# The head of a two-layer network as a third woven stream instead of four barriered phases

## The reference, cut to what matters

```python
x = L0_attn_x                                   # (8, 512, 128)
xn = _layernorm(x)
s = _L0_attn_ref(xn, Wq, Wk, Wv, Wo)            # causal attention, 16 heads, key width 8, value width 64
g = _silu(_L0_ffn_ref(xn, w_gate, c_fc, c_proj))# 8 experts, top 2, at most 512 tokens per expert
x = x + s * g
xn = _layernorm(x)
s = _L1_attn_ref(xn, ...)                       # delta rule in chunks of 32, mixed with an EMA
g = _silu(_L1_ffn_ref(xn, ...))                 # two layers of windowed attention and a gated ffn
x = x + s * g
```

## Time and profile before

| what | us |
|---|---|
| median of 3 runs (2751.47 to 2760.95) | 2754.06 |
| the profiled execution's own time | 2756.0 |
| its span, first to last instruction | 2754.2 |
| PE busy | 2051.2 (74%) |
| ACT busy | 1416.9 (51%) |
| DVE busy | 1352.0 (49%) |
| POOL busy | 532.1 (19%) |

### The profile page before, as it was taken

How to read it: one execution, slowest core, us unless ns; L and a number is a source line. 1 busy time by engine, 2 the same in 40 slices (tenths; PEclk the granted TensorE clock), 3 DMA queues, 4 the chain that set the end, 5 groups by cost and what they waited for, 6 DMA issues and landing times.

```text
span 2754.2 us, 51642 instructions
## 1 busy us (share of the span) xinstructions
PE 2051.2 (74%) x20756; PEld 1166.5 (42%) x20756; DVE 1352.0 (49%) x3140; ACT 1416.9 (51%) x3619; POOL 532.1 (19%) x601
## 2 busy tenths in 40 slices
PE   1405574779787978798878887898789787978767
PEld 0303223444453445344634463445444453445434
DVE  2512333554546463746474646555654546463442
ACT  0311361387537662776367735764477537762433
POOL 0270200312022110402040304020302022110220
PEclk9957776789888988898889897998889888988787
DMA  5362300200020001100020002000200020000000
GB/s 187 102 173 64 77 2 12 48 2 2 13 52 1 2 7 34 24 3 5 14 47 3 1 14 51 3 1 13 51 2 2 13 52 1 2 7 12 1 0 5
DMA packets 97224, 75.91 MB, mean 28 GB/s; under 512 B 44451, under 2 KB 87804, under 8 KB 94814
## 3 DMA queue, kind: packets, MB, share of 16 engines
q1 hardware_dynamic: 92894, 66.35, 9.7%
q0 software_dynamic: 4096, 6.32, 1.5%
HBM read 41.55 MB, written 33.16 MB: 27 GB/s over the span
## 4 chain that ended last, share of the span: by engine, by line
PE 45%; ACT 16%; DVE 14%; issue 8%; POOL 5%; DMA 1%; SPq 0%; POOLq 0%; DVEq 0%; ACTq 0%
PE PS L945 5%; PE PS L1581 4%; ACT work_a L1146 4%; PE PS L1616 4%; ACT work_b L1812 3%; PE PS L1718 3%; POOL work_b L2021 3%; DVE work_a L1265 3%; PE PS L1689 3%; PE PS L1731 2%; DVE work_a L1309 2%; PE PS L921 2%; PE PS L1651 2%; ACT work_a L1163 2%; PE PS L1680 2%
## 5 line engine op out<-in xcount | busy, mean ns | idle before, releaser
L1146 ACT ACTIVATE work_a<-PS,work_a 128x512 bf16<-128x512 f32 (+3 forms) x512 | 263.4, 530 | 79.3 <-DVE work_a L1265 77.8
L2021 POOL TENSOR_TENSOR work_b<-work_b,tables 128x256 f32<-128x256 f32 x256 | 212.0, 848 | 450.7 <-DVE work_b L1908 450.7
L1812 ACT ACTIVATE work_b<-PS,neg_max 128x192 f32<-128x192 f32 (+1 forms) x512 | 201.9, 417 | 121.1 <-DVE neg_max L1948 75.0
L1265 DVE TENSOR_REDUCE work_a<-PS 128x2 f32<-128x1024 f32 (+3 forms) x256 | 200.8, 821 | 106.5 <-PE PS L897 103.6
L1163 ACT ACTIVATE work_a<-PS 128x1024 f32<-128x1024 f32 (+1 forms) x192 | 169.6, 883 | 121.2 <-PE PS L927 119.1
L1581 PE MATMUL PS<-wqkv,hT 128*128 128x512 f32 x384 | 200.6, 654 | 7.5 <-DVE work_b L1908 6.2
L1616 PE MATMUL PS<-k,q 64*128 64x192 f32 (+1 forms) x1024 | 162.3, 454 | 58.7 <-ACT shiftT L1798 27.9
L2035 POOL TENSOR_TENSOR rstd_b<-var_eps_b,minus_half 128x4 f32<-128x4 f32 x16 | 16.4, 1027 | 876.1 <-DVE var_eps_b L121 876.1
L945 PE MATMUL PS<-work_a 128*64 128x512 f32 (+3 forms) x1024 | 179.8, 454 | 0.0
L1616 PEld LDWEIGHTS PS<-k,q 64*128 64x128 f32 x1024 | 109.7, 266 | 112.2 <-ACT work_b L1812 39.8
L1828 ACT ACTIVATE work_b<-PS 128x768 f32<-128x768 f32 (+1 forms) x128 | 97.2, 759 | 97.6 <-PE PS L1659 97.6
(11 more groups left out here) (295 smaller groups left out, 4218.4 us busy)
## 6 DMA issues: line engine op xcount, KB each, us to landing
work_a<-stack_d SPq DMA_DIRECT2D x32, 512.0 KB, 9.6
stack_d<-parts SPq DMA_DIRECT2D x48, 192.0 KB, 3.5
stack_d<-parts SPq DMA_DIRECT2D x32, 128.0 KB, 2.7
x_all<-in_L_attn_x_dram SPq DMA_DIRECT2D x4, 512.0 KB
slots_in<-xn_all SPq DMA_DIRECT2D x1, 2048.0 KB, 9.4
xnT_d<-xnT_all SPq DMA_DIRECT2D x1, 2048.0 KB
xn_all<-slots_in SPq DMA_DIRECT2D x8, 256.0 KB, 3.4
slots_out<-xn_all SPq DMA_DIRECT2D x8, 256.0 KB, 2.2
```

Source lines behind the costliest of these rows:

```text
L1146: nc.scalar.activation(dump0[:, n % 2 * T:n % 2 * T + (i + 1) * P], PS[:, a:a + (i + 1) * P], ACT.Exp, bias=neg_max0[:, k:k + 1], accum_ou ...
L1265: nc.vector.reduce_max(neg_max0[:, 2 * g * NT + i:(2 * g + 2) * NT:NT], at[:, :, Q_AT[i]:Q_AT[i] + (i + 1) * P], AX_X, negate=True).then_i ...
L1812: nc.scalar.activation(dump2[:, n % 4 * 256:n % 4 * 256 + w], PS[:, a:a + w], ACT.Exp, bias=neg_max2[:, k:k + 1], accum_out=sums2[:, k:k + ...
L2021: nc.gpsimd.tensor_tensor(to[:, n, :, r, :], src[:, n, :, 1 - r, :], table(2 * n + 1, t)[:, 32 * r:32 * r + 32].unsqueeze(1).to_broadcast( ...
```

## The change

- The barriers and the two loops go. Setup, norms, routing, scatter, stacks and experts are a third stream H of 45 slices: 1 of loads, 8 of norms (one batch each), 1, 3 of routing, 7 of stacks (batches 1 to 7), 1, and 24 of experts (three for each).
- H is woven with stream A of batch 0 by `HEAD_AHEAD`: slices 0 to 11 of H come first, then 30 slices of A (v, the whole first pass, unit 0 of the second), slice 12 of H, 4 of A, and then slices 13 to 20 of H with 1, 1, 1, 0, 1, 0, 4 slices of A ahead of slices 14 to 20. Slices 21 to 44, the experts, have one slice of A among them. Then A goes on with unit 14 of its second pass.
- SP loads x and five small tensors first, then clears, presets, and the other 43 loads. Batch 0's stack is written within the norms. The 2 MB store of `xnT_d` is split into batch 0 and the rest.
- The stack parts have two buffers instead of four; every batch's q and k go through banks 5 and 6 of PSUM instead of three pairs.
- For batch 0, the gather, its weighting and the additions move from the beginning of attention to behind its second pass, after all eight experts are stored, and gather into an area of its own.
- The conversions of masks and the rotary tables move from setup to slice 12 of H, behind the first 30 slices of A.
- `x1`, `y`, `out1` of the odd batches, and all of stream B's work area, share memory with the head.
- `A_AHEAD` has other values with the same sum; `A_AHEAD[0]` stays 17.
- The last barrier goes too.

```diff
+        FIRST_LOADS = [(cst[:, :], const_in[:, 0:C_LOOP]), (head_c[:, :], const_in[:, C_LOOP:C_COS]),
+                       (qk_in[:, 0:P], w_q0), (qk_in[:, P:2 * P], w_k0), (wg[:, :], w_gate)]
+        def head_sp(sp):
+            for q in range(4):
+                sp.dma_start(xn_all[...], x_in[...]).then_inc(sh["x_in_%d" % q], 16)
+                if q == 0:
+                    for dst, src in FIRST_LOADS:
+                        sp.dma_start(dst, src).then_inc(sh["loaded_first"], 16)
+            sp.wait_ge(sh["zeros"], 1)
+            for q in range(8):
+                sp.dma_start(slots_in.rearrange("(q p r) f -> q p (r f)", q=8, p=P)[q], zeros[:, :]
+                             ).then_inc(sh["cleared"], 16)
...
+            for dst, src in LOADS:
+                sp.dma_start(dst, src).then_inc(sh["loaded"], 16)
+            yield
...
+            for b in range(B):
+                if b == 1:
+                    sp.wait_ge(sh["T_copied"], 1)
+                    sp.dma_start(xnT_d[0:P, :], xnT_all[:, 0:T]).then_inc(sh["first_stored"], 16)
+                if b == 2:
+                    stacked(0)
+                yield
...
+            for b in range(1, B):
+                stacked(b)
+                yield
...
+            sp.wait_ge(sh["qk"], 2 * B)
+            sp.wait_ge(sh["xnT_stored"], 16)
+            for e in range(2):
+                weights(e)
+            for n in range(RING):
+                sp.wait_ge(stack_written[n], 16 * 12 * (B // RING))
+            sp.wait_ge(scattered, 16 * 2 * NTILE)
+            for e in range(2):
+                rows_of(e)
+            yield
...
+        def head_act(act):
+            def parts(b):
+                if b >= 2:
+                    act.wait_ge(stack_written[(b - 2) % RING], 16 * 12 * ((b - 2) // RING + 1))
...
+        def head_pool(gp):
...
+            gp.wait_ge(sh["slot"], 3)
+            gp.wait_ge(sh["cleared"], 16 * 9)
+            for n in range(NTILE):
+                for k in range(2):
+                    nc.gpsimd.indirect_dma_start(...).then_inc(scattered, 16)
+            gp.wait_ge(sh["converted"], 1)
...
         def attention_pool(gp, b):
...
             if b:
                 gp.wait_ge(sd["mixed"], ofd("mixed"))
+                gather()
...
+            for n in range(UNITS + 1):
+                yield
+            if b == 0:
+                gp.wait_ge(sh["stored"], 16 * NE)
+                gather()
+                weighted()
+                added()
...
         def attention_sp(sp, b):
+            if b == 0:
+                sp.wait_ge(sh["first_stored"], 16)
+                sp.wait_ge(sh["preset"], 64)
+            if b == 1:
+                sp.wait_ge(sh["xnT_stored"], 16)
+            sp.wait_ge(stack_written[b % RING], 16 * 12 * (b // RING + 1))
...
         A_LEAD = 76
-        A_AHEAD = (17, 0, 2, 1, 0, 0, 0, 0, 0, 4, 2, 0, 2, 0, 1, 0, 0, 0, 2, 2, 2, 1, 2, 1, 2, 1, 2, 2, 1, 6, 3, 0, 1, 1,
-                   1, 1, 2, 3, 1, 2, 1, 2, 1, 1, 1, 1, 0, 5, 1, 0, 1, 0, 1, 2, 0, 4, 0, 0, 0, 0, 0, 1, 1, 1, 0, 0, 1, 0)
+        A_AHEAD = (17, 0, 3, 1, 0, 0, 1, 0, 0, 2, 2, 1, 0, 2, 1, 0, 0, 0, 1, 2, 2, 1, 2, 2, 1, 2, 1, 2, 1, 3, 3, 0, 1, 1,
+                   1, 1, 1, 1, 3, 0, 3, 1, 1, 2, 2, 0, 1, 0, 1, 0, 1, 1, 2, 2, 1, 2, 2, 0, 2, 1, 1, 1, 0, 1, 1, 1, 0, 1)
+
+        HEAD_AHEAD = (0, 0, 0, 0, 0, 0, 0, 0, 0, 0, 0, 0, 30, 4, 1, 1, 1, 0, 1, 0, 4, 0, 0, 0, 0, 0, 0, 0, 0, 0, 0, 0, 0, 0,
+                      0, 0, 0, 0, 0, 0, 0, 0, 0, 1, 0)
```

## The result

The changed kernel takes 2685.48 us (median of four runs, 2665.45 to 2696.65), the kernel before 2756.37 beside it (four runs): a ratio of 0.9735, 95% interval 0.9672 to 0.9798. That is 71 us, or 2.6%, faster. Forecast were 2626, with a range of 2588 to 2672. The direction was right, the size about half of what was forecast, and the time lies outside the range.

The account below looks back on a forecast made before the run. No engine bounds the 517 us serial start; mostly PE bounds the eight woven periods. 2756.0 less 127.7 (head folded under batch 0) and 1.3 (last barrier), 0 for the new list: 2627, stated as 2626 us, range 2588 to 2672.

Parts of the forecast that it names:

- The new `A_AHEAD`: Seven woven periods: the new order of stream A's slices costs 0, bounds -5 and +5 us a period, -35 and +35 overall.
- the cover of the inverse's round trip through DRAM: Woven periods: only three stream B slices remain between the triangular inverse's steps and the product needing their DMA round trip.
- Loads 46, `slot_to` 62, scatter 64 to 146: Head: loads end at 46 us with norms hidden, routing gives `slot_to` at 62, POOL's scatter runs from 64 to 146.
- The rival of a late scatter on POOL: Head: DVE holds up the scatter's issues, 2.67 us each, ending at 235, 32 late: 2658 us; chance 0.06.
- Slice 12 costs 7: Head: PE and ACT wait 7 us for DVE's mask conversions and rotary tables, formerly hidden behind setup's presets.
- Stacks 8.94 each, ring just fits: Head: seven stack batches take 8.94 us each of SP's queue, 62.6 in all; two part buffers just suffice.
- Experts 6.6: Head: each of eight experts takes 6.6 us, 53 in all, from a first transpose at 207.5 to 265.
- `wo` 283.5, `x1` 292: Batch 0's end: `wo` starts at 283.5 us; the late gather costs 1 us, putting `x1` at 292 instead of 419.7.
- the three signs named: Would refute the forecast: stream B starting after 410 us, expert 0's transposes awaiting the scatter, or periods over 4 us from 288.
- Rival 5: Woven periods slow by more than the head gains, over 18.4 us each, awaiting the inverse's round trip: 2767 us; chance 0.03.
- The rule weighed: Scatter: by the skill's shared-port rule, 64 issues take 198 us, ending at 262 and adding 59 us; not used in the sum.
- the scatter lies beside it at no cost: Batch 0's first attention pass, 47.0 us: without head work on PE, ACT or DVE, it loses nothing to POOL's scatter.

Follow-up runs that it names:

- e13: The changed kernel with the old `A_AHEAD` list, the same code as e1 run again in a later series: 2618.29 us, ratio 0.9503.
- e3: The changed kernel with the new `A_AHEAD` values for its first 29 entries and the old ones behind: 2717.36 us, ratio 0.979.
- e4: The changed kernel with the old `A_AHEAD` values for its first 29 entries and the new ones behind: 2734.71 us, ratio 0.9859.
- e16: The changed kernel with its new `A_AHEAD`, but three slices of stream A moved from the 59th to 61st entries to the 30th: 2765.77 us, ratio 1.0041.
- e1: The changed kernel with the old `A_AHEAD` list, first run: 2682.42 us, ratio 0.9672.
- e5: The changed kernel, unchanged, run again in another series: 2749.89 us, ratio 0.9911.
- e7: The changed kernel with the old `A_AHEAD` and nine more slices of stream A beside the stacks: 2678.42 us, ratio 0.9668.
- e6: The changed kernel with the old `A_AHEAD` and the scatter's issues moved behind VectorE's tables: 2676.67 us, ratio 0.9664.
- e2: The kernel before the change with only the new `A_AHEAD` list put in: 2845.73 us, ratio 1.0258.
- e8: Probe: the changed kernel with the old `A_AHEAD` and only 2 of the scatter's 64 issues, experts computing on zeros: 2618.26 us, ratio 0.9456.

## Why the prediction was wrong

**The failed step is "The new `A_AHEAD` ... I take 0, with bounds of -5 and +5 us a period".** It costs 11.5 us a period, 80.5 us in all, over twice the upper bound. Undone alone (e13), the kernel takes 2618.29, 8 us under the forecast of 2626 and inside its own range.

What the 11.5 us are made of is seen in two whole stretches of seven periods, that of the changed kernel above and this one of e13:

```profile
378.30:2400.60 2022.30, 1673.39 (x17850) 954.83 (x17850) 1101.41 (x2465) 1197.92 (x3101) 401.38 (x455) 0.88 0.08 16
```

The same 17850 matmuls take (1723.99 - 1673.39) / 7 = 7.2 us more a period, and PE idles 53.9 instead of (2022.3 - 1673.4) / 7 = 49.8: 4.1 more. So about two thirds isn't waiting but slower matmuls. Most of that has a place: the last products of stream A's inverse, lines 672 and 682, and stream B's products of line 1382, part of which stand among them in PE's queue. Over the seven periods, the groups of instructions of e13:

```profile
L672 PE MATMUL PS<-work_a 32*32 32x32 f32 x896 | 19.1, 194 | 0.0
L682 PE MATMUL PS<-work_a 32*32 32x64 f32 x896 | 31.0, 217 | 4.0 <-DVE work_a L1012 4.0
L1382 PE MATMUL PS<-area_b,w_sb 128*128 128x512 f32 (+1 forms) x168 | 79.1, 607 | 6.1 <-ACT area_b L1504 6.1
```

and those of the changed kernel:

```profile
L672 PE MATMUL PS<-work_a 32*32 32x32 f32 x896 | 28.7, 236 | 1.8 <-DVE work_a L1006 1.8
L682 PE MATMUL PS<-work_a 32*32 32x64 f32 x896 | 44.2, 272 | 0.0
L1382 PE MATMUL PS<-area_b,w_sb 128*128 128x512 f32 (+1 forms) x168 | 100.7, 746 | 0.0
```

The inverse's two lines cost 22.8 us more in seven periods, 3.3 a period, and line 1382 another 21.6, 3.1 a period. Together that is 6.3 of the 7.2; the other lines differ both ways (line 1280 the most, 15.6 us less in seven periods) and nearly cancel. In the timeline of PE, first of e13, then of the changed kernel (second period each):

```profile
916.92 2.73 PE L672 MATMUL PS<-work_a 32*32 32x32 f32 x128
921.18 4.43 PE L682 MATMUL PS<-work_a 32*32 32x64 f32 x128 [0.57 <-DVE work_a L1012]
```

```profile
935.99 4.20 PE L672 MATMUL PS<-work_a 32*32 32x32 f32 x128 [0.23 <-DVE work_a L1006]
940.12 3.78 PE L1382 MATMUL PS<-area_b,w_sb 128*128 128x512 f32 x4
943.83 7.56 PE L682 MATMUL PS<-work_a 32*32 32x64 f32 x128
```

The same 256 products take 7.16 us and 11.76 us. The granted clock over them, by stretch, is 1.00 in e13 and 0.50 in the changed kernel, the 2.4 and the 1.2 GHz level:

```profile
917.00:926.00 9.00, 8.43 (x264) 7.91 (x264) 5.18 (x18) 0.76 (x2) 1.01 (x1) 1.00 0.01 4
```

```profile
936.00:952.00 16.00, 16.00 (x261) 13.04 (x262) 2.73 (x4) 3.11 (x4) 0.00 (x0) 0.50 0.01 3
```

So it is in four of the seven periods (second, third, sixth and seventh). In the other three the clock over these products is 0.67 to 0.76, and they take 8.3 to 8.8 us. Ahead of them, in the second period, PE had been busy 11.5 of 18.2 us in the changed kernel, with a wait of 5.31 us for stream B's line 1628 among them, and 17.2 of 18.3 us in e13. That this thinner stretch brought the lower clock is read from two traces side by side; no run changed it alone.

The prediction did name the cover of the inverse's round trip through DRAM, and the wait is there, in DVE's waits of the changed kernel over seven periods:

```profile
DVE work_a L996 <- DMA work_a<-low_d: 30.5, 7, 5.9
```

4.4 us a period, none in e13. ACT also loads a function table 19 times a period instead of 16, 1.28 us each. But what makes stream A late to begin with, 13 us at its gates (203.6 us into the period against 190.2), lies ahead of all this, and no run here places it: e3 and e4 put cost into both parts, and e16 shows that giving three slices back makes it worse, with PE's waits for the gates' inputs at 36.0 us in seven periods against 4.3. A single cause wasn't found. What is shown is that the cost is the list's, its size, and its split.

**Point by point.**
- *Loads 46, `slot_to` 62, scatter 64 to 146*: 47.3, 62.9, 64.07 to 147. Right; (146.15 - 64.07) / 63 = 1.30 us an issue. The rival of a late scatter on POOL didn't come. (The lower bound of the loads is 12.8 / 0.309 = 41.5 us, not 43; nothing hangs on it.)
- *First score 72, second pass 119*: 73.4 and 120.5.
- *Slice 12 costs 7*: PE waited 7.58. First part at 137: 138.4.
- *Stacks 8.94 each, ring just fits*: 55.7 us for seven, 8.0 each. The ring held: ACT waited for a landing five times, 15.7 us in all and 4.2 at most. 7 us better.
- *Experts 6.6*: (254.65 + 2.05 - 200.14) / 8 = 7.1 with the start, 6.3 between experts in the middle. First transpose 200.1, forecast 207.5.
- *`wo` 283.5, `x1` 292*: 274.4 and 281.9. *127.7 us less*: 137.8. The head's sum was 10 us too careful. In this run, and in series 3 and 4, the head folds as the prediction has it.
- *The last barrier, 1.3*: within the noise of the last stretch (216.2 before, 214.2 after).
- *What would make it wrong*: of the three signs named, the last came, a period that differs from 288 by over 4 us. In series 1 and 2 the first came too: with all 64 issues stream B began at 439 to 445, later than 410.
- *Rival 5*, slower periods, had the right direction. Its mechanism, waiting behind the inverse's round trip, is a part only: 4.4 us a period of DVE's waits, while PE's idle time grew by 4.1 and its matmuls by 7.2. Its threshold of 18.4 us wasn't reached, and the case between 5 and 18 us had been given no chance.
- *The rule weighed.* SBUF — State Buffer in the Trainium skill, section "SBUF: two separate sides", has POOL's descriptor writing wait while DVE runs an operation in a two-port mode. The prediction's estimate left this condition out and took all 64 issues at the long figure. The issues kept 1.30 us each here, and 1.28 in e1 beside its gaps. No run here shows the rule's effect; what slowed in two series was the other way round, and not DVE.

The head's gain has a condition that the prediction didn't see: "the scatter lies beside it at no cost" held in the first measurement and in series 3 and 4 only. In series 1 and 2 the gain was 62 to 66 us smaller in every kernel with the scatter beside the first pass, and the changed kernel was then only 0.9% faster than before (e5). The kernel before, whose scatter lies beside the stacks, lost less there: 2772.42 and 2768.87 against 2754.82 and 2754.56.

## What to carry to other kernels

A hand-tuned order is a part of the kernel with a price of its own: where it changes together with something else, cost it as unknown with wide bounds times the number of periods, and run the old order with the new code first; moving five slices at one entry cost 19.8 us a period. When a stage is hidden, look for the chain that was level with it: units moved out of the way brought `wo` 11 us forward and `x1` nothing, since the gather was next. The best kernels here were the new head with the old list (2618.29) and with nine units beside the stacks (2615.71), 5.0% faster than before and not told apart; in the series with gaps the same two were 3.3% faster (e1, e7).

## What the runs showed of the hardware that was not expected

While POOL issued the 64 indirect transfers, what waited for a product of PE started late in two of four series, by up to 31 us (e6), 68.0 us in seven waits in the first pass of e1. It set in some 15 us behind the first issue in e1 and ended 7 us behind the last. In one of these series SP's writes beside the scatter were slow too: 113 GB/s instead of 220 from 160 to 180 us, with PE's products long made (e2). POOL's own pace (1.28 us an issue in e1), ACT to DVE (0.04 us in e6) and ACT to PE (0.06 in e1) stayed as ever. With 2 issues there was none of it (e8). One chip showed it in one series and not in the next. What switches it on, whether PE's product or its signal is late, and whether slow writes and late products have one cause, is open.

The same 256 small matmuls took 7.2 us at a granted clock of 1.00 and 11.8 at 0.50. Which of the two they got changed with the order of slices alone; ahead of them PE had been busy 17.2 of 18.3 us in the one case and 11.5 of 18.2 in the other. That this is the cause was not tested.
